# Cross-attention and feed-forward on one core: values kept as head pairs in DRAM, first loads moved into the preparation, and a finish with shared small operations

## The reference

```python
q = (layernorm(x) @ Wq + bq)          # 2048 tokens, 16 heads of 32
k, v = cond @ Wkv + bkv               # 4 x 1601 = 6404 context rows of 512
q, k = fq_sym(q, axis=-1), fq_sym(k, axis=-1)      # max|.|/127 of each token and head
v = fq_sym(v, axis=2)                              # max|.|/127 of each channel, over all rows
attn = fq_unsigned(softmax(q @ k.T), axis=-1)      # 0..255
x = x + (attn @ v) @ Wp + bp
h = mx_linear(bf16(layernorm(bf16(x'))), W1, b1)   # x' = layernorm(x); blocks of 32: shared exponent
y = mx_linear(bf16(gelu(h)), W2, b2)               # 512 -> 2048 -> 512
x = x + bf16(bf16(x') + y)
```

## Time and profile before

| | |
|---|---|
| median of 3 runs | 2722.95 us |
| the profiled execution | 2737.58 us (its span 2735.8) |
| prepare, attention, finish in the span | to 553.6, to 2443, to 2735.8 |
| busy: TensorE, VectorE, ScalarE, GpSimd | 82%, 91%, 72%, 52% |
| granted TensorE clock | 0.821 of full speed |
| prepare: TensorE, VectorE busy | 498.5 and 420.5 of 553.6 us |
| attention: TensorE, VectorE busy | 1523.2 and 1829.4 of 1889.4 us |
| finish: TensorE, VectorE busy | 227.5 and 242.7 of 292.8 us |

### The profile page before, as it was taken

One profiled execution on the slowest core, in us unless ns is written; L12 is line 12 of the kernel. 1 busy time (PEld: TensorE's weight loads), 2 busy tenths in 40 slices (PEclk: granted clock), 3 DMA queues, 4 the chain that ended last, 5 costly groups with the idle time before them and its releaser, 6 DMA issues. The chain is left out here.

```text
span 2735.8 us, 52956 instructions
## 1 busy us (share of the span) xinstructions
PE 2249.1 (82%) x20003; PEld 1193.3 (44%) x20020; DVE 2492.6 (91%) x3592; ACT 1983.4 (72%) x1813; POOL 1419.5 (52%) x1855
## 2 busy tenths in 40 slices
PE   8899899968888888788888788888887777867886
PEld 4444454424444444444444444444444444433443
DVE  6998667879999999999999999999999999957997
ACT  3344333458888888888888888888988888864665
POOL 2432222136556575666757667675775758552001
PEclk9999999967677777777777876787777888779999
DMA  7565445489999999999999999999999999991000
GB/s 228 123 146 114 89 97 120 90 190 175 197 177 202 203 181 197 181 197 185 191 210 180 193 200 193 192 183 211 178 197 194 189 195 175 180 213 43 16 16 27
DMA packets 1389368, 442.13 MB, mean 162 GB/s; under 512 B 1323924, under 2 KB 1364372, under 8 KB 1387576
## 3 DMA queue, kind: packets, MB, share of 16 engines
q1 hardware_dynamic: 1378472, 397.08, 76.7%
q10 hardware_dynamic: 10736, 43.11, 6.3%
HBM read 78.99 MB, written 42.35 MB: 44 GB/s over the span
## 5 line engine op out<-in xcount | busy, mean ns | idle before, releaser
L888 DVE TENSOR_SCALAR_CACHE_REDUCE arena<-a_ps_s 128x1281 f32<-128x1281 f32 (+1 forms) x1280 | 1826.3, 1488 | 46.1 <-PE a_ps_s L833 38.1
L940 ACT ACTIVATE arena<-arena,a_bias,a_row_scale 128x3328 uint8<-128x3328 f32 (+1 forms) x512 | 1560.4, 3048 | 257.4 <-POOL a_bias L1003 255.7
L833 PE MATMUL a_ps_s<-arena,a_q_rep 96*128 96x512 bf16 (+2 forms) x3840 | 1232.4, 443 | 325.0 <-DVE arena L888 290.7
L846 PEld LDWEIGHTS a_ps_o<-a_v_head,a_nT 128*128 128x128 f16 x13056 | 529.6, 103 | 295.2 <-issue 160.9
L833 PEld LDWEIGHTS a_ps_s<-arena,a_q_rep 96*128 (+1 forms) x3840 | 314.6, 109 | 767.8 <-DVE arena L888 417.8
L1010 POOL CAST a_nT<-arena 128x1664 int16<-128x1664 uint8 x256 | 401.8, 1570 | 352.3 <-DMA arena<-arena 349.5
L846 PE MATMUL a_ps_o<-a_v_head,a_nT 128*128 128x32 f16 x13056 | 518.8, 183 | 43.4 <-POOL a_nT L1011 39.8
L1011 POOL CAST a_nT<-arena 128x1664 int16<-128x1664 uint8 x256 | 402.9, 1574 | 0.0
L358 POOL TENSOR_TENSOR p_rest<-p_kq,p_parts 128x512 f32<-128x512 f32 (+1 forms) x51 | 88.8, 1742 | 317.2 <-ACT p_parts L468 317.2
L999 POOL TENSOR_SCALAR a_row_max<-a_row_max,a_part_max 128x1 f32<-128x1 f32 x256 | 92.2, 360 | 246.6 <-DVE arena L888 229.3
L388 PE MATMUL p_ps_k<-p_wkv,p_ctxT 128*128 128x512 f32 (+1 forms) x408 | 190.3, 611 | 0.0
(11 more groups left out here) (151 smaller groups left out, 1943.0 us busy)
## 6 DMA issues: line engine op xcount, KB each, us to landing
k_parts_transposed<-p_stage SPq DMA_DIRECT2D x25, 768.0 KB, 7.0
p_ctx<-in_ctx_dram SPq DMA_DIRECT2D x25, 512.0 KB, 5.8
arena<-k_parts_transposed ACTq DMA_DIRECT2D x48, 240.1 KB, 4.0
late_values<-arena SPq DMA_DIRECT2D x51, 192.0 KB, 6.9
a_late_v<-late_values ACTq DMA_DIRECT2D x6, 1632.0 KB, 9.6
arena<-in_L_ffn_W_dram SPq DMA_DIRECT2D x8, 1024.0 KB, 8.1
arena<-k_parts_transposed ACTq DMA_DIRECT2D x48, 160.1 KB, 3.8
a_q_rep<-q_transposed ACTq DMA_DIRECT2D x48, 128.0 KB, 5.4
```

The source lines that it names most:

```text
L833: last = nc.tensor.matmul(ps_s[:, b, n0:n0 + w], q, k_parts[0:3 * HD, slot, start[c] + n0:start[c] + n0 + w], start=True, stop=True)
L846: last = nc.tensor.matmul(ps_o[:, u, 0:HD], nT[:, u, j, :], v_head[:, v_slot, j, :], start=(j == 0), stop=(j == KT - 1))
L888: nc.vector.tensor_scalar(s_row[:, u, start[c]:start[c] + size[c]], ps_s[:, (u + c) % 2, 0:size[c]], 1.0, None, ALU.mult, ALU.max, accum_o ...
L940: nc.scalar.activation(out, s_row[:, u, keys_of_half[half]], ACT.Exp, scale=row_scale[:, u, 0:1], bias=bias[:, u:u + 1], accum_out=zsum[:, ...
```

## The change

**Values.** `v32` goes. `take_values` writes into a ring of three tiles (`v_tile`, in the arena), and from tile 3 on it first waits until the store of tile t - 3 has landed (`v_stored[t % 3]`) and ScalarE has taken the absolute values of tile t - 3. All 8 head pairs of every tile are stored (256 KB for a tile where there were 192). ScalarE makes `vabs` between `hi` and `mid`; VectorE takes one maximum per tile, one tile late; `GROUPS` goes. `EARLY_HEADS` is 2 instead of 4: the first pair is loaded back after the last store and rounded by VectorE; the other 14 heads go through `round_values`.

**Early first loads.** The loads of keys for heads 0 and 1 and of half the queries of head 0 are issued by SP in prepare, ahead of the stores of queries 8 to 15; the other nine query loads come behind these stores. `q_rep`, `v_head` and `k_parts` are made ahead of prepare.

**Attention.** `round_values` does one operation in each of rows 3 to 14, ahead of the unpacking of that row. The first four tiles of x are loaded in the last head.

**Finish.** The bias of the projection becomes a fifth matmul over the three 16-bit parts of the bias (96 rows); `add_bias` goes. Powers of gated and hidden blocks are made by three operations of 80 columns where there were three of 64 and three of 16. The norm of the first tiles is split in two, and SP's loads come in another order.

```diff
+    v_tile = view(3 * C).rearrange("p (u c) -> p u c", c=C)
+    vabs = view(2 * C).rearrange("p (u c) -> p u c", c=C)
...
-            def store_late_values(t):
+            def store_values(t):
                 sp.wait_ge(v_taken, t + 1)
-                sp.dma_start(late_v_dram[:, :, place(t), :].rearrange("g p c -> p g c"),
-                             v32[:, place(t), EARLY_HEADS * HD:C].rearrange(
-                                 "p (g c) -> p g c", c=GROUP * HD)).then_inc(late_v_stored, 16)
+                sp.dma_start(v_dram[:, :, place(t), :].rearrange("g p c -> p g c"),
+                             v_tile[:, t % 3, :].rearrange("p (g c) -> p g c", c=GROUP * HD)).then_inc(v_stored[t % 3], 16)
...
             for t in range(2 * PAIRS - 2, KT):
-                store_late_values(t)
+                store_values(t)
+            for i in range(3):
+                sp.wait_ge(v_stored[i], 16 * ((KT + 2 - i) // 3))
...
+            sp.dma_start(v_first.rearrange("p t c -> p (t c)"),
+                         v_dram[0].rearrange("p t c -> p (t c)")).then_inc(v_first_loaded, 16)
...
+            load_keys(0)
+            for i in range(2):
+                sp.wait_ge(q_stored[i], 16 * (HALF_Q // 2))
+            load_queries(0, 0, head_loaded[0])
+            load_keys(1)
             for t in range(HALF_Q, QT):
-                if t > HALF_Q:
-                    store_query(t - 1)
-                for h in heads_beside(t):
-                    sp.wait_ge(v16_ready, h + 1)
-                    sp.dma_start(v_dram[h], v16[:, h % 2].rearrange("p t d -> p (t d)")).then_inc(v_stored[h % 2], 16)
-            store_query(QT - 1)
+                store_query(t)
             for i in range(2):
                 sp.wait_ge(q_stored[i], 16 * (QT // 2))
...
+            load_queries(0, 1, late_q_loaded[0])
+            for half in range(2):
+                load_queries(1, half, head_loaded[1] if half == 0 else late_q_loaded[1])
...
                 nc.scalar.activation(parts[0:r, 0, :], kq[0:r, :], ACT.Copy).then_inc(hi_ready, 1)
+                act.wait_ge(v_taken, t + 1)
+                after_first(act, vmax_done, t - 1)
+                nc.scalar.activation(vabs[0:r, t % 2, :], v_tile[0:r, t % 3, :], ACT.Abs).then_inc(vabs_ready, 1)
                 act.wait_ge(rest_ready, t + 1)
...
             def take_values(t):
                 r = rows(t)
-                if t == BIAS_TILE:
-                    dve.wait_ge(b_stored, 16)
-                if t == W_TILE:
-                    dve.wait_ge(w_turned, 2 * PIECES)
+                if t >= 3:
+                    dve.wait_ge(v_stored[t % 3], 16 * (t // 3))
+                    dve.wait_ge(vabs_ready, t - 2)
...
-            def largest_values(t):
-
-                for first, last in GROUPS.get(t, ()):
-                    some = v32[:, first:last, :].rearrange("p t c -> p c t")
-                    dve.wait_ge(v_taken, t + 1)
-                    steps.then_wait(nc.vector.tensor_reduce(largest[:], some, AX.X, ALU.max, apply_absolute_value=True))
-                    steps.then_wait(nc.vector.tensor_tensor(v_scale[:], v_scale[:], largest[:], ALU.max))
...
+            def largest_value(t):
+                r = rows(t)
+                dve.wait_ge(vabs_ready, t + 1)
+                after_first(dve, vmax_done, t)
+                nc.vector.tensor_tensor(v_scale[0:r, :], v_scale[0:r, :], vabs[0:r, t % 2, :],
+                                        ALU.max).then_inc(vmax_done, 1)
...
             for row in range(ROWS):
-                maximum_and_unpack(row, row % 2)
-                head, part = row // QT + 1, row % QT - ROUND_AT
-                if EARLY_HEADS <= head < H and 0 <= part < ROUND_PARTS:
-                    round_values(head, part)
+                maximum(row, row % 2)
+                head, step = row // QT + 1, row % QT - ROUND_AT
+                if EARLY_HEADS <= head < H and 0 <= step < 2 * ROUND_PARTS:
+                    round_values(head, step)
+                if row >= 1:
+                    unpack(row - 1, 1 - row % 2)
...
-            def add_bias(k):
-                if k % 4 == 0:
-                    pool.wait_ge(x_loaded[k // 4], 16)
-                nc.gpsimd.tensor_tensor(x1[:, k, :], x1[:, k, :], bp, ALU.add).then_inc(xb_ready, 1)
...
+                nc.tensor.matmul(ps_p[:], ones[:], parts[:, F + C:F + 2 * C], start=False, stop=True).then_inc(p_ready, 1)
...
+            def quantise(t, k, i):
+
+                if t is not None:
+                    largest_of_gated(t)
+                if i is not None:
+                    small(*i)
+                if k is not None:
+                    largest_of_hidden(k)
+                if t is not None or k is not None:
+                    powers(0 if t is not None else BF, BF + BC if k is not None else BF)
+                if t is not None:
+                    gated_integers(t)
+                if k is not None:
+                    hidden_integers(k)
```

More of the change, by code:

```diff
@@ L27 @@
 MX_FLOOR = 2.0 ** -119
-EARLY_HEADS = 4
 GROUP = 2
+EARLY_HEADS = GROUP
 class Steps:
@@ L94, with prepare @@
 WORDS = 13
-def prepare(nc, A, ident, identf, arena, scales, v_column, inv_v, q_dram, k_dram, v_dram, late_v_dram, weights):
+def prepare(nc, A, ident, identf, arena, scales, v_column, inv_v, q_dram, k_dram, v_dram, first, weights):
     K, T, C, F, H, HD = A.K, A.T, A.C, A.F, A.H, A.HD
@@ L1011, in unpack @@
                 nc.gpsimd.tensor_copy(high_T[u], bytes_T[:, u, :, 1]).then_inc(unpacked, 1)
-            def maximum_and_unpack(row, u):
-                maximum(row, u)
-                if not (isinstance(row, int) and row == 0):
-                    unpack(row - 1, 1 - u)
             def add_sums(h):
@@ L1058, in _, with finish @@
             pool.wait_ge(scaled, H)
-def finish(nc, A, identf, ident, arena, attn, wp, vectors, wp_loaded, weights, out):
+def finish(nc, A, identf, ident, arena, attn, wp, vectors, wp_loaded, x0_loaded, weights, out):
     T, C, F, H, HD = A.T, A.C, A.F, A.H, A.HD
@@ L1086, in finish @@
     w2 = w2T.rearrange("p (j o) -> p j o", o=C)
-    bp, ln_w, ln_b = (vectors[:, i, :] for i in range(3))
+    ln_w, ln_b = (vectors[:, i, :] for i in range(2))
     with Phase(nc, "f") as ph:
@@ L1367, in quantise_hidden, with powers @@
                 dve.wait_ge(h_ready, k + 1)
-                quantise(h[:, k % 2, :], h8[:], hq[:, k % 2, :], BC,
-                         lambda: after_first(dve, hT_ready, k - 1)).then_inc(hq_ready, 1)
-                dve.wait_ge(hq_ready, k + 1)
+                steps.then_wait(nc.vector.tensor_reduce(power[:, BF:BF + BC], blocks(h[:, k % 2, :]), AX.X, ALU.max,
+                                                        apply_absolute_value=True))
+            def powers(first, last):
+                p, v, f, e = (ap[:, first:last] for ap in (power, inverse, floor, exponent))
+                steps.then_wait(nc.vector.tensor_tensor(p, p, f, ALU.max))
+                steps.then_wait(nc.vector.tensor_tensor(p.bitcast(I32), p.bitcast(I32), e, ALU.bitwise_and))
+                steps.then_wait(nc.vector.tensor_tensor(v.bitcast(I32), p.bitcast(I32), e, ALU.bitwise_xor))
@@ L1396, in moments_of_residual, with variance, small @@
                 steps.value += 1
[L1398 removed]
+            def variance(i, first, last):
                 dve.wait_ge(steps_sem, steps.value)
[L1400 to L1408 removed]
+                nc.vector.tensor_tensor(var_eps[:, i % 2, first:last], mv[:, i % 2, first:last, 1], eps[:, first:last],
+                                        ALU.add).then_inc(var_ready, 1)
+            def small(i, first, last):
+                s, n = i % 2, norms.index((i, first, last))
+                mean = mv[:, s, first:last, 0]
+                a, r, v, scale = (ap[:, s, first:last] for ap in (rec, root, var_eps, rstd))
+                dve.wait_ge(var_ready, n + 1)
+                dve.wait_ge(root_ready, n + 1)
                 steps.then_wait(nc.vector.reciprocal(a, r))
```

339 lines of the change are left out of this document (175 added, 164 removed).

## The result

The changed kernel takes **2773.52 us** (median of 4, 2765.21 to 2780.56) against 2724.80 of the kernel before: a ratio of 1.0179 (95%: 1.0146 to 1.0212), so +49 us. Measured once more it took 2762.25 against 2726.69, 1.0122 (1.0094 to 1.0150), +36 us. The forecast was 2744, with a range up to 2770: the sign was right, the size was not.

What follows compares the result with a forecast made beforehand. Prepare was taken as bound by TensorE late and VectorE from 100 to 200, attention by VectorE. The terms 21 - 9 + 12 + 6 + 0 - 9 = +21 on 2722.95 gave 2744 us, range 2704 to 2770.

Steps and rivals of the forecast that it cites:

- The value ring: Prepare: VectorE waits at odd tiles for a store of values to land; +21 first stretch, +12 last.
- The landing taken: Prepare: time for a 256 KB store of values to land, 7.1 us late and 7.9 from 90 to 253.
- The middle stretch: Prepare, 11th to 19th store of keys: slack in the loop, long reductions give way to tile maxima; -9 us.
- The end of prepare: Prepare into attention: early loads delay the last queries by 10 us, save 9.7, nine query loads cost 4; +6.
- Attention: Attention: same transfers, spread rounding goes into GpSimd's waits; 0, between -10 and +8 us.
- the one on the finish: Finish: -6 us for its start, -3 for shared powers with a fifth matmul; together -9, between -15 and -3.
- Stores in time: Rival, prepare: stores land in time and the ring costs nothing; 2699 us, chance 0.17.
- A clock that falls: Rival, TensorE: idling in every pair lowers its granted clock, as from 100 to 200; 2773 us, chance 0.08.
- That the rounding decides attention: Rival, attention: rounding ahead of unpacking makes scores wait, +34 us with a free ring; 2733 us, chance 0.07.

Runs made afterwards that it cites:

- the experiment with the values first: Changed kernel, ring of three, with SP issuing both stores of values ahead of the store of keys in each pair: 2725.20 us, 0.9987.
- two experiments: Changed kernel with five value tiles instead of three, 2722.48 us (0.9981); changed kernel with stores of values issued before keys, 2725.20 us (0.9987).

## Why the prediction was wrong in size

**What held.** *The value ring* did what was worked out: VectorE stands at `take_values` for odd tiles alone, 14 times where 16 were counted, TensorE waits from 450 to 500 (44.66 busy of 50), and the loop over a pair sets the pace: on average the last six pairs took 17.2 and 17.8 us in the two traces against 18.25 worked out, the first ten 20.5 and 21.1 against 20.45. The landing taken, 7.1 and 7.9, was too long (6.5 and 7.1 in the first trace, 5.7 and 6.4 in the second). The middle stretch has no such wait and gained 8 to 13 where -9 stood (its working slips: eight pairs are 16 tiles and not 20, and half of 30 - 14 is 8; with 16 tiles the half is 9). Up to the last store of keys it is +24.0 and +19.3 together, against +24. Taking the wait away is worth 38 us by the runs, since the gain of the maxima then shows. The prediction hung its rivals on the landing; the experiment with the values first shows that the late issue behind the store of keys, which its loop has too, weighs more. *The end of prepare* was right in its parts: query 8's store late by over 10 us, attention's wait gone, nine issues more; +4.9 and +2.6 against +6. *Attention* was taken at 0; in its traces it varies from 1869 to 1884 us with no pattern by kernel that I can name (1868.9 and 1884.1 with the same code of attention), and the 1881.6 before lies within that, so the first trace's -12.7 shows no gain.

**The step that failed** is the one on the finish: "The powers cost 3 x (0.222 + 0.174) = 1.19 us a tile before; three of 80 columns at some 0.23 save 0.5 to 0.6 a tile", and from it -3, with -6 for its start. The start was right: from the start of the block to the first output tile it is 75.5 us (2460.2 to 2535.7) against 81.1 before, -5.6, and 74.2 to 78.7 in the other traces, and the 128x4 operations are down to 0.18 at most. The operations on the powers cost what was said (0.24 each). But I priced them as work on VectorE, and read the order in which they now stand as neutral. To share the powers, the hidden tile's three operations (2.2 us) must stand ahead of the gated tile's integers, and these feed a loop of their own: TensorE's down projection, ScalarE's copy, the hidden turn behind it, the square roots, and VectorE again. I had even read that TensorE's chain was close behind VectorE, and used it to make the gain smaller, not to ask what a later release does to it. The term was -9 and measured +12.2 and +14.0, a miss of 21 to 23 us; with the order put back, finish is 285.1 to 291.0 in four traces, against 290.9 before and 303.1 to 304.9 in the eight traces with the changed order. With the measured term the sum would have been 2765 to 2767, within the range and 3 to 8 from the two medians.

**The rest of the miss** lies in carrying one execution over to medians, and its cause is not shown. The kernel before was traced at 14.6 us above its median and the changed one at 8.3 below; the second trace of the changed one was 3.7 above its own. Between traces the difference is +27.6, between medians +49 and +36. That +27.6 comes near the +21 is luck: finish was off by +21 and attention by -13, and they nearly cancel.

**The rivals.** Stores in time was ruled out for the change and true for two experiments. A clock that falls was wrong: the granted clock is 0.831 where it was 0.821, in prepare 0.96 where it was 0.97, and 0.94 from 100 to 200 where it was 0.93. That the rounding decides attention was wrong (2700.0 and 2700.2 with and without the spread). None of the rivals was the one that happened, a finish that gets slower from its order; it belonged on the list.

## What to carry to other kernels

A ring of buffers whose writer waits for a DMA store closes a loop over issue, queue and landing; count that loop from one issue to the next before counting the work that it saves, and if it is longer than the bound engine's period, add buffers or issue the waited-for store first (both took all of it away here, for 38 and 37 us; the second because the store then left 14 to 18 us sooner). When operations of two tiles are merged to save small ones, ask what the first tile's result now waits for: 0.5 us saved a tile put 2.2 us of delay on a chain between three engines, and cost some 17 us in all. Loads moved ahead of stores that something waits for only move the wait; between those stores, where nothing waited for them, the end of prepare was 3 us shorter than with them behind (48.0 to 48.2 in three traces, 51.2 in two), too little for the medians to show.

## What was not expected of the hardware

Landing times followed neither the bytes nor the place in the queue alone. Stores of 256 KB landed in a median of 3.9 us from 448 to 500 with nothing of their pair ahead, and in 5.4 to 6.5 behind a 768 KB store; but from 90 to 253 it was 6.5 ahead of that store and 6.1 to 7.1 behind it. A 512 KB load put in between added at most 0.7. The same code had landings of 6.5 and 5.7 us in two executions in its late stretch, and its first stretch took 211.1 and 205.5.
